# SyncE's large loads in an attention kernel: four, six or more at the start of a pass, or one to three in each of its slots

## The reference

```python
x = x + attention(LN1(x) @ w_qkv, mask_1) @ w_ao            # self-attention, 16 heads of 32
x = x + attention(LN2(x) @ w_q, ctx @ w_kv, mask_2) @ w_co  # cross-attention on the context
x = x + gelu(LN3(x) @ w1 + b1) @ w2 + b2                    # 512 -> 2048 -> 512
# non-local block: theta, phi, g are 1x1 convolutions, phi and g of the context
W = einsum('bnc,bcm->bnm', theta(x), phi(ctx)) / 512
out = batchnorm(conv(einsum('bnm,bmc->bnc', W, g(ctx)))) + x
attention(q, k, v, m) = softmax((q k^T / sqrt(32)) * m - 10000 * (1 - m)) v
```

## Time and profile before

| | |
|---|---|
| runs of before | 2138.86, 2139.02, 2142.21 us; median 2139.02 us |
| the profiled execution | 2140.79 us, span 2138.9 us |
| TensorE busy | 2092.2 us, 98% |
| VectorE, ScalarE, GpSimd busy | 67%, 55%, 20% |
| TensorE's mean granted clock | 0.996 |
| DMA, mean share of the 16 engines | about 20%, 67 GB/s |

### The profile page before, as it was taken

One profiled execution on the slowest core, in us unless ns is written; L12 is line 12 of the kernel. 1 busy time (PEld: TensorE's weight loads), 2 busy tenths in 40 slices (PEclk: granted clock), 3 DMA queues, 4 the chain that ended last, 5 costly groups with the idle time before them and its releaser, 6 DMA issues. The chain is left out here.

```text
span 2138.9 us, 43342 instructions
## 1 busy us (share of the span) xinstructions
PE 2092.2 (98%) x14434; PEld 1657.3 (77%) x14434; DVE 1433.6 (67%) x3823; ACT 1171.5 (55%) x3270; POOL 419.1 (20%) x388
## 2 busy tenths in 40 slices
PE   8989999999999999999999998999999999999998
PEld 7867777777777777777777776778888888888887
DVE  7688878888878788888888889565243343435233
ACT  4377877777777777777777777522111111112111
POOL 1001111011014133132122220143030321313000
PEclk9999999999999999999999999999999999999999
DMA  8411121121131231231221232321101010101001
GB/s 276 144 45 46 54 76 35 55 75 44 51 107 61 90 120 46 76 100 48 84 87 62 70 103 74 109 97 45 39 25 44 20 44 25 44 34 44 22 23 45
DMA packets 126451, 143.78 MB, mean 67 GB/s; under 512 B 23888, under 2 KB 74192, under 8 KB 126288
## 3 DMA queue, kind: packets, MB, share of 16 engines
q1 hardware_dynamic: 126288, 141.80, 20.4%
HBM read 113.94 MB, written 27.79 MB: 66 GB/s over the span
## 5 line engine op out<-in xcount | busy, mean ns | idle before, releaser
L1127 ACT ACTIVATE A_p<-A_p,A_nmax 128x256 f32<-128x256 f32 x1024 | 509.0, 507 | 0.0
L1395 DVE TENSOR_TENSOR A_p<-A_sc,A_mk 128x1024 f32<-128x1024 f32 x256 | 312.6, 1221 | 142.8 <-PE A_tp L893 142.8
L1405 DVE CUSTOM_DVE_ANT_0 A_p<-A_p,A_ma 128x256 f32<-128x256 f32 x1024 | 387.5, 435 | 6.1 <-DVE A_p L1395 0.5
L1133 ACT ACTIVATE A_pt<-A_tp 128x512 f32<-128x512 f32 x512 | 277.2, 593 | 178.7 <-PE A_tp L893 178.2
L893 PEld LDWEIGHTS A_tp<-A_ident,A_p 128*128 128x128 f32 x2048 | 229.9, 141 | 73.3 <-issue 51.0
L893 PE MATMUL A_tp<-A_ident,A_p 128*128 128x128 f32 x2048 | 274.2, 277 | 1.7 <-ACT A_pt L1133 1.4
L1127 ACT ACTIVATION_READ_ACCUMULATOR A_p<-A_p,A_nmax 128x1 f32 x1024 | 202.8, 198 | 0.0
L1251 ACT ACTIVATE A_mk<-A_tp,A_cols 128x512 f32<-128x512 f32 x62 | 42.6, 687 | 276.9 <-PE A_tp L68 276.9
L1251 ACT ACTIVATE A_ma<-A_tp,A_cols 128x512 f32<-128x512 f32 x62 | 42.6, 687 | 247.4 <-PE A_tp L68 247.4
L66 PE MATMUL A_banks<-A_xt_h,A_w_h 128*128 128x512 f32 x384 | 162.3, 423 | 6.6 <-DVE A_k_l L1379 5.1
L680 POOL TENSOR_TENSOR A_res<-A_res,A_o_bias 128x512 f32<-128x512 f32 x64 | 82.5, 1310 | 353.3 <-DVE A_nmax L1405 208.3
(11 more groups left out here) (231 smaller groups left out, 4899.0 us busy)
## 6 DMA issues: line engine op xcount, KB each, us to landing
A_x<-x SPq DMA_DIRECT2D x96, 256.0 KB, 4.1
A_res<-x SPq DMA_DIRECT2D x64, 256.0 KB, 2.8
A_rt<-inverses SPq DMA_DIRECT2D x512, 32.0 KB, 1.9
x<-A_res SPq DMA_DIRECT2D x64, 256.0 KB, 2.1
A_e<-ctx SPq DMA_DIRECT2D x16, 512.0 KB, 4.6
inverses<-A_turned_inv SPq DMA_DIRECT2D x512, 1.0 KB
A_e<-ctx_t SPq DMA_DIRECT2D x16, 512.0 KB, 6.6
A_e<-L_xattn_w SPq DMA_DIRECT2D x32, 256.0 KB, 3.2
```

Source lines behind the costliest of these rows:

```text
L1127: act.activation(p[:, g % 2, j, t, :], p[:, g % 2, j, t, :], ACT.Exp, scale=-1.0, bias=nmax[:, g % 2, j, t:t + 1], accum_out=rsum[:, g % 2 ...
L1133: act.activation(pt[:, j, :, :], tp[:, j % 2, :].rearrange("p (c s) -> p c s", c=TPB), ACT.Copy)\
L1395: dve.tensor_tensor(p[:, g % 2, heads, :, :].rearrange("p j t s -> p j (t s)"), sc[:, heads, :], m, ALU.mult)\
L1405: dve.tensor_tensor_reduce(out=a_, in0=a_, in1=ma[:, b, t, :], scale=-1.0, scalar=BIG, op0=ALU.add, op1=ALU.min, accum_out=nmax[:, g % 2, ...
```

## The change

SyncE's large loads are issued in other slots. Row tile t goes to slot t of the same body, the two context halves to slots 1 and 2, the mask of h = 0 to slot 7 of the body before, the weight chunks two a slot to slots 3 to 7 of body 7, slot 0, 5 and 6 of body 8, and ahead of the slot's stores. The MLP's first four chunks go to slots 1 and 2 of body 15 and its two vectors to slot 3. Sizes, number, users and waits of all transfers stay, and on TensorE, VectorE, ScalarE and GpSimd no instruction moves. The lines of after stand one or two lower than those of before.

```diff
+        load_at = {(7, 3): (0, 1), (7, 4): (2, 3), (7, 5): (4, 5), (7, 6): (6, 7), (7, 7): (8, 9), (8, 0): (10, 11),
+                   (8, 5): (12, 13), (8, 6): (14, 15)}
...
-            def load_rows(k, r):
-                for t in range(TT):
+            def load_rows(k, r, some=range(TT)):
+                for t in some:
                     wait(sp, x_lo, (r - 1) * TT + (t + 1))
                     sp.dma_start(x[:, t, :], row_tile(0, k, r, t)).then_inc(ld_x[t], DMA)
...
-                if h == 0:
-                    if k < NU:
-                        load_rows(k + 1, r + 1)
-                    if NB <= k + 1 < NU:
-                        load_context(r + 1)
-                    if NB < k < NU:
-                        load_mask(r, 0)
-                    for n in {7: range(0, 4), 8: range(10, 12)}.get(k, ()):
-                        load_chunk(n)
-                    if k == NU - 1:
-                        for n in range(4):
-                            load_m_chunk(n)
-                        sp.wait_ge(res_ok, NB * TT)
-                        sp.dma_start(ln_scale, across(ln_s)).then_inc(ld_ln, DMA)
-                        sp.dma_start(ln_shift[:, :], across(ln_b)).then_inc(ld_ln, DMA)
+                if h < TT and k < NU:
+                    load_rows(k + 1, r + 1, (h,))
+                if h in (1, 2) and NB <= k + 1 < NU:
+                    load_context(r + 1, h - 1)
                 if h == 3 and NB <= k < NU:
                     load_mask(r, 1)
+                if h == 7 and NB <= k < NU - 1:
+                    load_mask(r + 1, 0)
...
+                for n in load_at.get((k, h), ()):
+                    load_chunk(n)
                 if h == (5 if k < NU else 3) and k:
                     for t in range(2):
                         store(k - 1, r - 1, t)
-                if h == 5:
-                    for n in {7: range(4, 8), 8: range(12, 16)}.get(k, ()):
-                        load_chunk(n)
...
-                    for n in {7: range(8, 10)}.get(k, ()):
-                        load_chunk(n)
```

More of the change, by code:

```diff
@@ L447, in load_chunk, with load_context @@
                 sp.dma_start(wst[:, n % KT, :], x_weights[c][t * P:(t + 1) * P, :]).then_inc(ld_s[n % KT], DMA)
-            def load_rows(k, r):
-                for t in range(TT):
+            def load_rows(k, r, some=range(TT)):
+                for t in some:
                     wait(sp, x_lo, (r - 1) * TT + (t + 1))
                     sp.dma_start(x[:, t, :], row_tile(0, k, r, t)).then_inc(ld_x[t], DMA)
[L454 to L458, removed]
+            def load_context(r, b):
+                wait(sp, et_lo, (r - (NB + 1)) * BPB + (b + 1))
+                sp.wait_ge(ctx_lo, B)
+                sp.dma_start(e[:, b, :, :], ctx_d[(r - NB) * BPB + b]).then_inc(ld_e[b], DMA)
             def load_mask(r, b):
@@ L589, in slot @@
                     load_turned_w(3 * KT + 2)
-                if h == 0:
-                    if k < NU:
-                        load_rows(k + 1, r + 1)
-                    if NB <= k + 1 < NU:
-                        load_context(r + 1)
-                    if NB < k < NU:
-                        load_mask(r, 0)
-                    for n in {7: range(0, 4), 8: range(10, 12)}.get(k, ()):
-                        load_chunk(n)
-                    if k == NU - 1:
-                        for n in range(4):
-                            load_m_chunk(n)
-                        sp.wait_ge(res_ok, NB * TT)
-                        sp.dma_start(ln_scale, across(ln_s)).then_inc(ld_ln, DMA)
-                        sp.dma_start(ln_shift[:, :], across(ln_b)).then_inc(ld_ln, DMA)
+                if h < TT and k < NU:
+                    load_rows(k + 1, r + 1, (h,))
+                if h in (1, 2) and NB <= k + 1 < NU:
+                    load_context(r + 1, h - 1)
                 if h == 3 and NB <= k < NU:
                     load_mask(r, 1)
+                if h == 7 and NB <= k < NU - 1:
+                    load_mask(r + 1, 0)
+                if k == NU - 1 and h == 3:
+                    sp.wait_ge(res_ok, NB * TT)
+                    sp.dma_start(ln_scale, across(ln_s)).then_inc(ld_ln, DMA)
+                    sp.dma_start(ln_shift[:, :], across(ln_b)).then_inc(ld_ln, DMA)
+                for n in load_at.get((k, h), ()):
+                    load_chunk(n)
                 if h == (5 if k < NU else 3) and k:
@@ L609, in slot @@
                         store(k - 1, r - 1, t)
-                if h == 5:
-                    for n in {7: range(4, 8), 8: range(12, 16)}.get(k, ()):
-                        load_chunk(n)
[L613 to L616, removed]
-                    for n in {7: range(8, 10)}.get(k, ()):
-                        load_chunk(n)
-                for n in {(15, 5): (4,), (15, 6): (5,), (15, 7): (6, 7), (16, 1): (8,), (16, 2): (9,), (16, 3): (10,),
-                          (16, 4): (11,)}.get((k, h), ()):
+                if h == (7 if k < NU else 5) and k:
+                    for t in range(2):
+                        store(k - 1, r - 1, t + 2)
+                for n in {(15, 1): (0, 1), (15, 2): (2, 3), (15, 5): (4,), (15, 6): (5,), (15, 7): (6, 7), (16, 1): (8,),
+                          (16, 2): (9,), (16, 3): (10,), (16, 4): (11,)}.get((k, h), ()):
                     load_m_chunk(n)
```

## The result

The changed kernel took 2120.32 us (median of 4 runs, 2116.53 to 2121.58), the kernel before 2139.24 us (4 runs, 2138.86 to 2142.21): a ratio of 0.9906 with a 95% interval of 0.9888 to 0.9923. A second comparison on another occasion gave 2120.73 us (5 runs, 2117.76 to 2121.59) against 2137.7 us, 0.9924 (0.991 to 0.9937). The forecast was 2118.0 us with 2115 to 2121 as its own range. The gain is 18.9 us where 21 were forecast, and 17.0 us in the second comparison.

A forecast was written before the change was run, and what follows sets the result against it. TensorE bounds the kernel (busy 2092.2 of 2138.9 us). Terms of 7.29, 11.77 and 2.87 us make 21.93, taken as 21: 2139.02 - 21.0 = 2118.0 us, range 2115 to 2121 (8 in 10: 2114.5 to 2125.5).

The forecast's parts named there:

- The mechanism: SyncE's queue: slot 1's small inverse stores lie behind slot 0's large loads, so VectorE's L1422 waits, 18.5 us in all.
- at no cost: Row tiles, context halves, mask and weight chunks move to other slots with enough cover, so none costs time.
- Bodies 8 to 14: Seven bodies, 550.56 us against 7 x 76.97 = 538.79: 11.77 us to be gained.
- up to 1 us aside: Bodies 7 to 9: splits of 16 chunks stay and may own up to one microsecond of the 21.9 us.
- Body 15, slots 1 to 3: Slots 1 to 3 take 21.67 us against 18.80 in body 5: 2.87 us to be gained.
- Body 7: 84.26 us against 76.97: 7.29 us to be gained, from delayed inverses and a chunk waiting for GpSimd in slot 5.
- I take this stall as gone too: Body 7: earlier residual loads end TensorE's 2.08 us wait and the clock's dip; if not, about 4.9 us come back.
- The covers: Moved loads still land before their readers; row tiles, issued one slot ahead, have 5.5 us to spare.
- Rival 1: GpSimd's moved splits and mask additions fall on VectorE's maxima; 5 us stay, time near 2123 us; chance 0.10.
- Rival 2: Body 7's stall stays, as SyncE waits for GpSimd's splits in slots 6 and 7; 4.9 us back, 2123; chance 0.05.
- Rivals 3 and 4: Slots 1 and 2, bodies 7 to 14: delay moved there, 2133 us (0.05), or at full price, 2164 us (0.04).
- Rival 4: Full 2.87 us lost per slot, decided at a store-to-load distance between 3.2 and 6.8 us; 2164 us; chance 0.04.

The follow-up runs named there:

- the repeat: The kernel after again, unchanged, five rounds: 2120.73 us against 2137.7 us for before, ratio 0.9924.
- the dose: After with all row tiles back in slot 0, plus one context half (2121.94 us, one run) or both (2124.3 us, ratio to before 0.9939).

## Why the prediction was right, and where it was not

**The mechanism** was right as far as it went, and tested from both sides. The wait of L1422 vanished as forecast (under 2 us), and the distances are 2.3 to 3.1 us where at most 3.5 was said; the one of all slots that is over it, 4.25 us, is that of the inverses behind the result stores and two weight loads of body 15's slot 7, without a wait. Quarter-sized loads give the same distances without moving anything, and loads put back bring the waits back.

It was not the whole. The prediction moves the mask "at no cost" and gives all of body 9's excess to the inverses. But the mask, late behind the same loads, threw GpSimd's work onto VectorE's maxima, and with chunk splits in it that cost 2.68 us in body 9 where no inverses were waited for. That the sum came out all the same is no proof of its one cause: it was read from the bodies' lengths, which hold both, and the change takes away both.

**The sum**, term by term:
- Bodies 8 to 14: 11.16 of 11.77 us. The 0.61 us is in body 8 (77.35 us) and body 10 (77.19 us); the other five take 76.97 us. Body 8's part is in its slot 3 (9.76 instead of 9.38 us), with the chunk splits, for which the prediction had set up to 1 us aside; body 10's is in slot 6 and is absent from the repeat (76.97 us).
- Body 15, slots 1 to 3: 2.87 of 2.87 us, 18.80 us as in body 5.
- Body 7: 6.07 of 7.29 us. Its slots 1 and 2 gave 11.17 + 10.05 - 18.80 = 2.42 us, the estimate having been 2.4. Slot 6 fell from 14.94 to 10.29 us, 4.65 us. But slot 7, 9.39 us before, now takes 10.38: VectorE's result, behind its split and behind operations that GpSimd's work has stretched, had slack as long as TensorE was late itself, and is now what it waits for. So the stall of slots 5 to 7 was worth 3.65 us net where 4.9 was put. The step that was mis-sized is "I take this stall as gone too": it went, and it uncovered a microsecond beneath it.
- Body 15, the rest: 0.81 us of loss that had no term. It is all in the last slot, 8.40 us before and 9.21 now, in which the profile of after shows the clock at 0.50 (1307.82 to 1311.23). Before, the stretch at 0.50 began at 1329.30, where body 16 begins. That the clock is the reason is read from its place only; in the repeat this slot took 8.76 us, with as long a stretch at 0.50. A term for this could not be read from one execution.

Together 1.22 + 0.61 + 0.81 = 2.64 us missing from 21.93; the prediction set 0.93 aside. Against the median, 2.3 us too low, with 0.2 us from the other median of before.

**The covers** held. 5.5 us for the row tiles was right in kind: nothing waits in after, and a slot later VectorE waits 59 times with 4.7 us as the longest. The advice to issue a DMA early (the Trainium skill, "DMA: Bandwidth & Descriptors", "Rules for kernel authors") is thus borne out by that run. But once the loads land in time, still earlier gains nothing here, and it delayed a small transfer behind them.

**The rivals.** Rival 1's mechanism is real and went the other way. The argument against it, that the stretched maximum of the earlier trace rows stood in a body that was already late, was wrong: where body 9 was not held up by the inverses, GpSimd's late work stretched three maxima, and the change removed that. What is left of it is the likeliest reason for the last microsecond of body 7. Rival 2 did not happen: the residuals went out at 673.12, earlier than the 675.8 forecast. Rivals 3 and 4 put a loss into slots 1 and 2 behind three loads; the dose shows that eight cost bodies 9 to 14 nothing. Rival 4's edge, set between distances of 3.2 and 6.8 us, lies at some 6.1 where the loads land in 3.15 us, and lower where they take longer: a wait was seen at 5.1, a loss of time at 5.75.

**TensorE's idle time** fell by 15.3 us (15 or more was said), and in body 7 no lowered clock is left.

## What to carry to other kernels

- A small round trip on a queue (store, wait, load back) pays for the bytes issued ahead of it. Read the time from the store's issue to the landing of what is loaded back and compare it with the time at which the consumer wants it (9.3 us here); large loads that can go behind it, should, as long as each still lands before its reader.
- Look for every reader behind the same queue, not only for the one with the longest wait. The mask's reader, GpSimd, bounds nothing, but its late work fell on VectorE's and cost 2.68 us in one body.
- Price such a change by the length of a repeated body with the disturbance against one without, not by the sum of waits: here waits of 18.5 and 6.3 us stood for 19.3 us of time, and the undisturbed body of 76.97 us gave a bound that came out 2.6 us high.
- Where one body has two stalls, ask what the second covers. Taking away 4.65 us of a stall uncovered a microsecond that had been hidden beneath it.

## What was not expected of the hardware

- In two profiled executions of the same kernel TensorE's granted clock differed at the same places (0.50 or 1.00 around 140 us and 1317 us), 20.5 against 10.2 us at the lower level of 1.2 GHz in total, and the spans differed by 3.8 us. The runs of this kernel spread over 5 us; bodies 1 to 14 of the two traces agreed within 0.3 us, so the start and the end of the attention, with the clock in them, are where the two differ. The profiles of all the kernels here had between 10.2 and 30.7 us at 0.50.
- One VectorE operation was stretched from 0.73 to 2.41 us under a GpSimd operation of 2.35 us, and one from 0.42 to 1.50 us under one of 1.45 us: each took slightly longer than the GpSimd operation it met and ended 0.3 to 0.5 us after it.
- The delay of a small store grew with the bytes ahead of it, but not by them alone. From the store's to the load's issue it was 2.26 us at three loads in after, 4.3 to 5.5 us at eight (2 MB) in bodies 9 to 14 but 3.55 in body 7, 5.4 to 6.6 us at ten, 6.6 to 7.4 us at eleven in before but 6.05 to 6.54 with the chunks moved, 6.79 us at fourteen. That fourteen were no slower than eleven stays unexplained.
